# Gathers of the experts' rows on GpSimd: when a group of gathers waits for an earlier group to land

## Chip, core and metric

The kernel runs on one core of a Trainium2 chip. The metric is the device time of one execution in microseconds (us). Three runs of the kernel before gave 585.29 us as their median.

## What is computed

x has 8 sequences of 256 tokens with 128 features, 2048 tokens in all. Four layers are added to x, each on its layer norm: a state-space mixer, a routed feed-forward layer, a selective scan (Mamba), and the same routed feed-forward layer once more. Cut to what matters here:

```
x = x + attn_a(layernorm(x), ...)          # state-space mixer
x = x + ffn(layernorm(x), ...)             # first routed layer, t = 0 in the kernel
x = x + attn_b(layernorm(x), ...)          # selective scan
x = x + ffn(layernorm(x), ...)             # last routed layer, t = 1

def ffn(h):                                # 16 experts, each token takes the best one
    score = sigmoid(max over experts of h @ router.T), only for that expert
    routed = for each token: expert(score * h), expert = silu(gate) * up, then down
    shared = (silu(h @ shared_gate.T) * (h @ shared_up.T)) @ shared_down.T
    return shared + routed
```

## The kernel before

x stays in SBUF as 16 blocks of 128 tokens; four blocks are a group (group 0 to 3). Each engine has its own program, written out by hand in the order in which it runs, and engines wait for one another on named semaphores. Nothing reorders it.

A routed layer (`experts`, once with t = 0 and once with t = 1) goes like this:

- GpSimd (POOL in the profile) scatters each token's scaled row to an HBM tensor `by_expert`, in which the rows of an expert stand together in slots. These are indirect DMAs, one for each block of 128 tokens (`send`, L1821), four in a row for a group.
- SyncE and ScalarE fetch the slots, TensorE runs the experts on them (L736, L751, L763), and the results go back to `by_expert` as SyncE's and ScalarE's DMAs (L1970, L1604).
- When the last of them has landed (`put_back`), GpSimd gathers the rows back into the order of the tokens: 16 indirect DMAs at L1858, one for each block, in the loop `for g in GROUPS`. Each group of four has a semaphore of its own, `read_back[g]`. Before groups 2 and 3 GpSimd waits for the group two ahead (L1856).
- Beside that, the shared part runs. TensorE projects a group to gate and up (`project`, L699), ScalarE takes the gate through silu (L1554), VectorE multiplies it with up (L1178), TensorE projects down (`down`, L712), and VectorE adds the result to x (`add_shared`, L1184). `land` (L1244, VectorE) waits for `read_back[g]` and adds a gathered group to x.

What stands around the gathers differs between the two layers.

- First routed layer, on the way into the scan (`enter_scan`): VectorE does `land(0)`, the layer norm of group 0, `add_shared(2)`, the first piece of the shared part of group 3, `land(1)`, `land(2)` and then the other pieces. TensorE does `down(2)`, the transposes of group 0 (L446), one piece of group 3 (L699), and the 16 matmuls of the scan's input projection (`project_u`, L800), which wait for ScalarE to copy the transposed group (L1426). The last gathered group is added by GpSimd itself in the scan (`land_last`, L1897). Behind the gathers GpSimd has the products of the scan's steps (L1904).
- Last routed layer (`leave`): VectorE does `add_shared(2)`, the pieces of group 3, `land(1)`, `land(2)`, `add_shared(3)`, `land(3)`; SyncE writes a group out after each `land` (L1975). Nothing stands behind the gathers on GpSimd.

Of the kernel before, what the change touches and what calls it, by code (L numbers as in the profile page):

```python
# [15 lines left out]
GB = BANK // P  # L16
# [103 lines left out]
def build(nc, x_in, w_in, c_in, out):  # L120
    with ExitStack() as stack:
# [6 lines left out]
        def signal(name, events, step=1):  # L128
            return Signal(sem(name), events, step)

        pe, dve, act, pool, sp = (Queue(e) for e in (nc.tensor, nc.vector, nc.scalar, nc.gpsimd, nc.sync))
# [18 lines left out]
        def wt(name, rows=slice(0, P)):  # L150
            at, width = W_AT[name]
            return w[rows, at:at + width]
# [5 lines left out]
        def register(engine, place, below):  # L158

            return nc.values_load(place, engines=(engine,), min_val=0, max_val=below - 1,  # L160
                                  skip_runtime_bounds_check_because="the slots of all experts are fewer than the blocks")
# [21 lines left out]
        def blocks(g):  # L183
            return range(GB * g, GB * g + GB)
# [207 lines left out]
        read_back = [signal(f"read_back{g}", [(t, j) for t in TURNS for j in blocks(g)], 16) for g in GROUPS]  # L392
# [1390 lines left out]
        def gpsimd_program():  # L1783
# [17 lines left out]
            def hold_score(n, g):  # L1801

                js = slice(GB * g, GB * g + GB)
                pool.wait_ge(*score_exp[n, g])
                nc.gpsimd.tensor_scalar(score[:, js], score[:, js], 1.0, 3e38, ALU.add, ALU.min).then_inc(*score_held.inc((n, g)))

            def scale_rows(n, g):
                js = slice(GB * g, GB * g + GB)
                pool.wait_ge(*scores_ready[n, g])
                pool.wait_ge(*turned[n, g])  # L1810
                nc.gpsimd.tensor_tensor(xn[:, js, :], xn[:, js, :], score[:, js].unsqueeze(2).to_broadcast([P, GB, DM]),
                                        ALU.mult).then_inc(*rows_scaled.inc((n, g)))

            def send(n, js):

                g = js[0] // GB
                pool.wait_ge(*placed[n, g])
                pool.wait_ge(*rows_scaled[n, g])
                pool.wait_ge(*filled[len(fills) - 1])
                for j in js:  # L1820
                    nc.gpsimd.indirect_dma_start(by_expert, bass.IndirectOffsetOnAxis(position[:, j:j + 1], 0),  # L1821
                                                 xn[:, j, :], None).then_inc(*scatter[n // 2].inc(j))

            def experts(t, entry):
                n = 1 + 2 * t
                hold_score(n, NGRP - 1)
                scale_rows(n, NGRP - 1)
                send(n, blocks(NGRP - 1))
                for mark in entry:
                    pool.wait_ge(*mark)  # L1830

                def choose_weights(k):

                    if k >= 3:
                        pool.wait_ge(*expanded[t, k - 3])
                    s = pairs[k][1]
                    e = register(mybir.EngineType.Pool, expert_int[s:s + 1, 0:1], NE)
                    nc.gpsimd.tensor_copy(chosen[s % len(chosen)], wt("gate_up")[:, bass.ds(e * (2 * EF), 2 * EF)]).then_inc(*second_chosen.inc((t, k)))  # L1838

                whole_pairs = [k for k in range(n_pairs) if len(pairs[k]) == 2]  # L1840
                pool.wait_ge(*expert_ready[t])
                for k in whole_pairs[0:3]:
                    choose_weights(k)
                if t == 0:
                    pool.wait_ge(*taps_loaded[0])
                    pool.wait_ge(*load_late["w"])
                    nc.gpsimd.tensor_tensor(taps, taps, wt("in_b")[:, 0:DI].unsqueeze(1).to_broadcast([P, DC, DI]),
                                            ALU.mult).then_inc(*taps_ready.inc(0))
                    nc.gpsimd.tensor_tensor(past, ident.unsqueeze(1).to_broadcast([P, NCH, P]),
                                            wt("d_b").unsqueeze(2).to_broadcast([P, NCH, P]), ALU.mult).then_inc(*past_ready.inc(0))  # L1850
                for k in whole_pairs[3:]:
                    choose_weights(k)
                pool.wait_ge(*put_back[t][back[-1]])
                for g in GROUPS:
                    if g >= 2:
                        pool.wait_ge(*read_back[g - 2][t, GB * (g - 1) - 1])  # L1856
                    for j in blocks(g):
                        nc.gpsimd.indirect_dma_start(gathered[:, j, :], None, by_expert,  # L1858
                                                     bass.IndirectOffsetOnAxis(position[:, j:j + 1], 0)).then_inc(*read_back[g].inc((t, j)))
# [15 lines left out]
            for g in range(NGRP - 1):  # L1875
                if g >= 1:
                    hold_score(1, g)
                scale_rows(1, g)
                send(1, blocks(g))
            experts(0, exit_a)  # L1880

            def drive(g):
# [16 lines left out]
            for s in range(n_steps + 1):  # L1899
# [9 lines left out]
                for what, g in due_in_steps(s):  # L1909
# [10 lines left out]
                    elif what == "send 1":  # L1920
                        send(3, blocks(g)[1:GB])
            experts(1, exit_b)


# [151 lines left out]
```

## Time and profile before

| what | us |
|---|---|
| median of three runs (lowest, highest) | 585.29 (580.48, 586.97) |
| the profiled execution | 589.76 |
| its span, first to last instruction | 588.4 |
| outside the span | 1.4 |
| TensorE busy in the span | 480.0 (82%) |
| VectorE busy | 407.8 (69%) |
| ScalarE busy | 314.7 (53%) |
| GpSimd busy | 319.8 (54%) |

The mean granted TensorE clock over the span is 0.916 of full speed (2.4 GHz). The table tells how busy an engine is, not what bounds a stretch; for that the stretches with the gathers (205 to 254 us and 550 us to the end) have to be read row by row.

### The profile page before, as it was taken

What the parts mean: (1) busy time and instruction counts of PE and PEld (TensorE: products, weight loads), DVE (VectorE), ACT (ScalarE), POOL (GpSimd) and SP (SyncE); (2) the same over time, 40 slices, a digit from 0 to 9 for tenths busy, and PEclk for the clock granted to TensorE, in tenths of its full rate; (3) what the DMA queues carried; (4) which work ended last, traced back from release to release, by engine and by line L of the source; (5) the groups of instructions that cost most, each with busy time, mean ns of one, the idle gap of its engine ahead of it and who ended that gap; (6) DMA issues with size and microseconds to landing.
All of it is one profiled execution on the core that took longest, in us unless ns stands there. A gap on an engine that the chain in (4) does not pass through costs nothing.

```text
span 588.4 us, 7447 instructions
## 1 busy us (share of the span) xinstructions
PE 480.0 (82%) x2128; PEld 276.2 (47%) x2128; DVE 407.8 (69%) x821; ACT 314.7 (53%) x655; POOL 319.8 (54%) x298
## 2 busy tenths in 40 slices
PE   3987878988789984899788997887778677899936
PEld 1744446565459951363233443333324233489614
DVE  4588692974453333299999799999997997544303
ACT  2573656454435530557665885978386641646200
POOL 1059541553452172046789669897989666411450
PEclk9898996997898996989997998999798899899976
DMA  8999920000033410154555354566465630043321
GB/s 299 410 324 326 319 78 0 2 20 18 19 103 110 122 49 22 43 146 140 160 156 143 111 154 114 163 144 184 112 168 138 161 109 20 19 113 112 85 60 53
DMA packets 39991, 73.94 MB, mean 126 GB/s; under 512 B 4368, under 2 KB 20240, under 8 KB 39184
## 3 DMA queue, kind: packets, MB, share of 16 engines
q1 hardware_dynamic: 35600, 67.00, 38.0%
q0 software_dynamic: 2048, 4.20, 2.5%
q10 hardware_dynamic: 2304, 2.29, 1.2%
q8 instruction: 17, 0.28, 0.2%
q14 instruction: 22, 0.18, 0.1%
HBM read 66.00 MB, written 26.28 MB: 157 GB/s over the span
## 4 chain that ended last, share of the span: by engine, by line
PE 33%; DVE 24%; issue 15%; ACT 12%; POOL 8%; another core or an unknown queue 5%; DMA 2%; SPq 1%; DVEq 0%; POOLq 0%; ACTq 0%
DVE arena L1313 9%; PE psum L699 5%; PE psum L751 5%; POOL arena L1904 4%; PE psum L881 3%; PE psum L712 3%; PE psum L763 2%; PE psum L800 2%; DVE psum L1307 2%; ACT L1391 2%; ACT arena L1712 2%; ACT xn L1421 2%; PE psum L457 1%; POOL by_expert L1821 1%
## 5 line engine op out<-in xcount | busy, mean ns | idle before, releaser
L1904 POOL TENSOR_TENSOR arena<-arena 128x512 f32<-128x512 f32 x127 | 158.3, 1271 | 68.0 <-DVE arena L1313 67.7
L881 PE MATMUL psum<-arena,w 128*128 128x512 f32 x256 | 136.4, 652 | 27.8 <-POOL arena L1904 25.8
L1313 DVE TENSOR_TENSOR_SCAN arena<-arena,psum 128x512 f32<-128x512 f32 x128 | 148.4, 1200 | 8.3 <-ACT arena L1712 4.8
L1712 ACT ACTIVATE arena<-arena 128x510 f32<-128x510 f32 x128 | 87.2, 713 | 41.9 <-DVE arena L1313 39.5
L881 PEld LDWEIGHTS psum<-arena,w 128*128 128x128 f32 x256 | 46.6, 201 | 102.8 <-POOL arena L1904 76.4
L1307 DVE TENSOR_TENSOR psum<-psum,arena 128x512 f32<-128x512 f32 x128 | 81.5, 681 | 1.1 <-DMA arena<-bc_store 1.0
L699 PE MATMUL psum<-xnt,w 128*128 128x512 f32 x128 | 64.2, 651 | 10.2 <-ACT arena L1554 10.2
L1789 POOL TENSOR_TENSOR arena<-arena 128x512 f32<-128x512 f32 x16 | 20.7, 1295 | 69.6 <-DVE arena L1014 69.6
L1858 POOL DMA_INDIRECT arena<-by_expert,routes x32 | 30.6, 956 | 29.8 <-DMA by_expert<-arena 20.6
L699 PEld LDWEIGHTS psum<-xnt,w 128*128 128x128 f32 x128 | 25.5, 208 | 39.4 <-issue 27.5
L1821 POOL DMA_INDIRECT by_expert<-xn,routes x32 | 33.7, 1053 | 14.3 <-issue 7.9
L800 PE MATMUL psum<-xnt,arena 128*128 128x512 f32 (+3 forms) x64 | 33.1, 651 | 9.3 <-ACT xnt L1426 9.3
L1178 DVE TENSOR_TENSOR arena<-psum,arena 128x512 f32<-128x512 f32 x24 | 16.3, 689 | 34.9 <-PE psum L699 21.9
L1554 ACT ACTIVATE arena<-psum 128x512 f32<-128x512 f32 x24 | 14.2, 595 | 43.5 <-PE psum L699 18.4
L1391 ACT ACT_TABLE_LOAD x24 | 30.8, 1283 | 10.5 <-DMA c<-c_in 8.8
L751 PE MATMUL psum<-arena 128*128 128x128 f32 x248 | 34.3, 283 | 2.4 <-issue 2.4
L712 PEld LDWEIGHTS psum<-w,arena 128*128 128x128 f32 x256 | 33.1, 210 | 6.5 <-issue 6.5
L712 PE MATMUL psum<-w,arena 128*128 128x128 f32 x256 | 33.4, 293 | 1.8 <-DVE arena L1178 1.8
L1233 DVE TENSOR_TENSOR arena<-psum,arena 128x256 f32<-128x256 f32 (+1 forms) x32 | 13.3, 416 | 28.5 <-PE psum L763 18.1
L751 PEld LDWEIGHTS psum<-arena 128*128 128x128 f32 x248 | 31.5, 199 | 2.8 <-issue 2.8
L1838 POOL COPY arena<-w 128x256 f32 x30 | 11.8, 402 | 36.6 <-PE psum L751 36.6
L1184 DVE TENSOR_TENSOR x<-psum,x 128x512 f32<-128x512 f32 x7 | 4.8, 689 | 34.5 <-remote 26.2
(199 smaller groups left out, 826.8 us busy)
## 6 DMA issues: line engine op xcount, KB each, us to landing
arena<-bc_store SPq DMA_DIRECT2D x64, 512.0 KB, 4.9
by_expert<-w_in SPq DMA_DIRECT2D x4, 4096.0 KB, 43.4
w<-w_in SPq DMA_DIRECT2D x1, 4427.5 KB, 13.4
by_expert<-arena SPq DMA_DIRECT2D x56, 64.0 KB, 1.6
arena<-by_expert SPq DMA_DIRECT2D x54, 64.0 KB, 2.0
by_expert<-w_in SPq DMA_DIRECT2D x1, 1984.0 KB, 66.8
x<-x_in SPq DMA_DIRECT2D x4, 256.0 KB, 7.5
out<-x SPq DMA_DIRECT2D x4, 256.0 KB
```

The source lines that it names most:

```text
L699: nc.tensor.matmul(b, weights[:, P * c:P * c + P], xnt_group(g), start=True, stop=True).then_inc(*made.inc((t, g, c)))
L712: r = nc.tensor.matmul(b[:, P * q:P * q + P], act_of(t, g)[:, c, P * q:P * q + P], wt("shared_down")[:, DM * c:DM * c + DM], start=(c == 0 ...
L751: r = nc.tensor.matmul(b[:, P * (2 * q + half):P * (2 * q + half) + P], chosen[s % len(chosen)][:, EF * half:EF * half + EF], xs_t[:, P * ...
L800: r = nc.tensor.matmul(by_sequence(b)[:, :, back:SEQ], taps[:, DC - 1 - back, P * c:P * c + P], by_sequence(xnt_group(g))[:, :, 0:SEQ - ba ...
L881: nc.tensor.matmul(bank(6 + c), ident, state[c][s % 3], start=False, stop=(n == DS - 1)).then_inc(*summed.inc((s, c)))
L1307: nc.vector.tensor_tensor(bank(2 + c), bank(c), bc_row[i][:, 0, :], ALU.mult).then_inc(*driven.inc((s, c)))
L1313: nc.vector.tensor_tensor_scan(state[c][s % 3], decay_b[c][s % 2], bank(2 + c), 0.0, ALU.mult, ALU.add).then_inc(*state_ready.inc((s, c)))
L1391: nc.scalar.preload_act_table_set(name)
L1712: nc.scalar.activation(live, seq, ACT.Exp, scale=a_neg[:, DS * c + n:DS * c + n + 1]).then_inc(*decay_ready.inc((s, c)))
L1821: nc.gpsimd.indirect_dma_start(by_expert, bass.IndirectOffsetOnAxis(position[:, j:j + 1], 0), xn[:, j, :], None).then_inc(*scatter[n // 2] ...
L1858: nc.gpsimd.indirect_dma_start(gathered[:, j, :], None, by_expert, bass.IndirectOffsetOnAxis(position[:, j:j + 1], 0)).then_inc(*read_back ...
L1904: nc.gpsimd.tensor_tensor(state[c][s % 3], state[c][s % 3], bc_row[s % len(bc_row)][:, 1, :], ALU.mult).then_inc(*y_done.inc((s, c)))
```

## The change

Two lines of GpSimd's program differ:

```diff
                 for g in GROUPS:
-                    if g >= 2:
-                        pool.wait_ge(*read_back[g - 2][t, GB * (g - 1) - 1])
+                    if g == 2 or (g and t == 0):
+                        pool.wait_ge(*read_back[g - 1][t, GB * g - 1])
                     for j in blocks(g):
```

In the first routed layer each of groups 1, 2 and 3 now waits for the group just ahead of it. In the last one only group 2 waits, for group 1. No instruction is added, removed or moved on any engine but for these waits.

On GpSimd, in the first routed layer, between the last copy of an expert's weights and the first product of the scan; `put_back0` is the landing of the experts' results, `read_back0` to `read_back2` are the landings of gathered groups 0 to 2:

```order
 L1858 DMA arena<-by_expert,routes 128x128 [waits put_back0]
-L1858 DMA arena<-by_expert,routes 128x128 x7
+L1858 DMA arena<-by_expert,routes 128x128 x3
 L1858 DMA arena<-by_expert,routes 128x128 [waits read_back0]
 L1858 DMA arena<-by_expert,routes 128x128 x3
 L1858 DMA arena<-by_expert,routes 128x128 [waits read_back1]
 L1858 DMA arena<-by_expert,routes 128x128 x3
+L1858 DMA arena<-by_expert,routes 128x128 [waits read_back2]
+L1858 DMA arena<-by_expert,routes 128x128 x3
 L1904 TENSOR_TENSOR arena<-arena 128x512 [waits bc_loaded0,state_ready]
```

The wait for group 0 has moved from the ninth gather to the fifth, that for group 1 from the thirteenth to the ninth, and there is a new one for group 2 at the thirteenth.

On GpSimd, in the last routed layer, to the end of its program:

```order
 L1858 DMA arena<-by_expert,routes 128x128 [waits put_back1]
 L1858 DMA arena<-by_expert,routes 128x128 x7
-L1858 DMA arena<-by_expert,routes 128x128 [waits read_back0]
-L1858 DMA arena<-by_expert,routes 128x128 x3
 L1858 DMA arena<-by_expert,routes 128x128 [waits read_back1]
-L1858 DMA arena<-by_expert,routes 128x128 x3
+L1858 DMA arena<-by_expert,routes 128x128 x7
```

Here the ninth gather waits for group 1 (the eight ahead of it) rather than for group 0, and the thirteenth waits for nothing.

## Rows read from the trace of the kernel before

**Rows 1.** The chain that ended last, its shares of the span by engine.
```profile
PE 33%; DVE 24%; issue 15%; ACT 12%; POOL 8%; another core or an unknown queue 5%; DMA 2%; SPq 1%; DVEq 0%; POOLq 0%; ACTq 0%
```
**Rows 2.** The same chain in order of time, its longest pieces: start us, us, what.
```profile
217.58 10.95 another core or an unknown queue
...
556.03 17.36 another core or an unknown queue
```
**Rows 3.** Waits: engine and line, waited for: us in total, times, longest us.
```profile
DVE x L1184 <- remote: 26.2, 2, 15.1
...
ACT arena L1554 <- remote: 16.8, 1, 16.8
...
ACT xnt L1426 <- remote: 11.0, 1, 11.0
```
**Rows 4.** TensorE in order of time, first routed layer: start us, us, what [idle before <-releaser].
```profile
213.94 3.81 PE L712 MATMUL psum<-w,arena 128*128 128x128 f32 x32 [0.88 <-DVE arena L1178]
217.58 0.60 PE L446 MATMUL psum<-w,xn 128*128 128x128 f32 x4
218.02 1.88 PE L699 MATMUL psum<-xnt,w 128*128 128x512 f32 x4
229.21 9.91 PE L800 MATMUL psum<-xnt,arena 128*128 128x512 f32 x16 [9.30 <-ACT xnt L1426]
```
**Rows 5.** VectorE and ScalarE in order of time, first routed layer.
```profile
228.50 0.69 DVE L1184 TENSOR_TENSOR x<-psum,x 128x512 f32<-128x512 f32 x1 [11.07 <-remote]
...
228.56 0.60 ACT L1426 ACTIVATE xnt<-psum 128x512 f32<-128x512 f32 x1 [10.97 <-remote]
```
**Rows 6.** GpSimd in order of time, first routed layer: gathers 1, 9 and 16.
```profile
205.68 1.02 POOL L1858 DMA_INDIRECT arena<-by_expert,routes  x1 [8.89 <-DMA by_expert<-arena]
...
215.84 0.95 POOL L1858 DMA_INDIRECT arena<-by_expert,routes  x1 [0.30 <-issue]
...
224.65 0.95 POOL L1858 DMA_INDIRECT arena<-by_expert,routes  x1 [0.30 <-issue]
```
**Rows 7.** GpSimd in order of time, last routed layer: gathers 4, 8 and 16.
```profile
554.38 0.95 POOL L1858 DMA_INDIRECT arena<-by_expert,routes  x1 [0.30 <-issue]
...
559.40 0.95 POOL L1858 DMA_INDIRECT arena<-by_expert,routes  x1 [0.30 <-issue]
...
569.43 0.95 POOL L1858 DMA_INDIRECT arena<-by_expert,routes  x1 [0.30 <-issue]
```
**Rows 8.** VectorE in order of time, last routed layer.
```profile
556.96 0.69 DVE L1244 TENSOR_TENSOR x<-x,arena 128x512 f32<-128x512 f32 x1 [1.11 <-DMA arena<-by_expert,routes]
557.57 0.68 DVE L1178 TENSOR_TENSOR arena<-psum,arena 128x512 f32<-128x512 f32 x1
573.37 0.69 DVE L1184 TENSOR_TENSOR x<-psum,x 128x512 f32<-128x512 f32 x1 [15.12 <-remote]
...
585.43 0.69 DVE L1244 TENSOR_TENSOR x<-x,arena 128x512 f32<-128x512 f32 x1
```
**Rows 9.** TensorE in order of time, last routed layer.
```profile
556.67 3.73 PE L712 MATMUL psum<-w,arena 128*128 128x128 f32 x32
560.24 3.60 PE L699 MATMUL psum<-xnt,w 128*128 128x512 f32 x8
...
578.72 5.88 PE L712 MATMUL psum<-w,arena 128*128 128x128 f32 x32 [0.88 <-DVE arena L1178]
```
**Rows 10.** The scatters, whole span: line engine op, count | busy us, mean ns | idle before.
```profile
L1821 POOL DMA_INDIRECT by_expert<-xn,routes x32 | 33.7, 1053 | 14.3 <-issue 7.9
```
**Rows 11.** GpSimd in order of time: the third group of four scatters, its first and last.
```profile
150.06 1.06 POOL L1821 DMA_INDIRECT by_expert<-xn,routes  x1 [1.62 <-DVE routes L1002]
...
153.97 0.97 POOL L1821 DMA_INDIRECT by_expert<-xn,routes  x1 [0.30 <-issue]
```
**Rows 12.** Stretches: us, busy PE PEld DVE ACT POOL, clock, DMA share, GB/s.
```profile
220.00:228.00 8.00, 0.00 (x0) 0.00 (x0) 0.00 (x0) 0.00 (x0) 4.39 (x5) 0.79 0.20 49
228.00:236.00 8.00, 6.79 (x10) 2.90 (x11) 5.07 (x20) 1.34 (x3) 0.00 (x0) 0.57 0.00 0
```

## The prediction

> **What bounds the kernel now.** I read the page first. The busy shares name TensorE, but the chain that ended last holds a term that belongs to no engine: 5% of the span is put down to "another core or an unknown queue" [rows 1]. On one core that is strange. In order of time almost all of it is two pieces, 10.95 us from 217.58 and 17.36 us from 556.03 [rows 2], and both lie inside the two stretches in which GpSimd issues its 16 gathers, 205.68 to 225.60 and 550.57 to 570.38 [rows 6, 7]. The list of waits has only three lines that end "remote", and they are the same two places [rows 3].
>
> Then the first stretch engine by engine. TensorE ends `down(2)` at 213.94 + 3.81 = 217.75 and the transposes of group 0 at 218.18 [rows 4]. VectorE's `add_shared(2)` waits for nothing but that `down(2)`, and ScalarE's copy for nothing but those transposes; they start at 228.50 and 228.56 [rows 5]. So 10.7 and 10.4 us pass between the end of the work and the start of whoever waits for it. From 220 to 228 TensorE, VectorE and ScalarE run no instruction at all, while GpSimd goes on; the DMA engines are busy for only 0.20 of the time [rows 12]. The second stretch is a copy of it: TensorE ends `down(2)` at 560.40 and runs eight more matmuls to 563.84 [rows 9]; VectorE's L1184 starts at 573.37 [rows 8], 13.0 us after its input.
>
> What do the two have in common? Both are let go a fixed time after the gathers: 228.50 is 2.90 us after the last gather's end in the first layer (224.65 + 0.95 = 225.60), 573.37 is 2.99 us after it in the last (569.43 + 0.95 = 570.38). A gather lands about 2.58 us after its start: the fourth gather starts at 554.38 and `land(0)`, which waits for it, starts at 556.96 [rows 7, 8]. So the release comes 1.3 to 1.4 us after the last landing. My reading: **while a long unbroken train of gathers runs, TensorE's signals reach nobody**, and they are given out when the train has drained. When it sets in can be bounded. TensorE's result at 556.8 (L699, just before the `down` of rows 9) still reached VectorE at 557.57 [rows 8], when six gathers had been started; the result at 560.40 did not come through, with the eighth just done and the ninth due at 560.65. In the first layer the result at 217.75 was held, after gather 9 at 215.84 [rows 6].
>
> Trains of four show nothing of the kind. The 32 scatters are the same kind of instruction of the same length, 1053 ns [rows 10], in groups of at most four with several us between groups (one is 150.06 to 154.94 [rows 11]); no wait in the whole profile ends "remote" beside them [rows 3].
>
> **The change, part by part.** The old waits never bind: gather 9, which has one, follows at the usual 0.30 us [rows 6]. So nothing is gained from their removal. A new wait binds each time, as the group just ahead has not landed. Gathers stand 1.26 us apart ((224.65 - 205.68) / 15); with a wait the next one starts 2.58 us plus about 0.07 us after the one ahead. Each new wait costs GpSimd 2.65 - 1.26 = 1.4 us: 4.2 us for three in the first layer, 1.4 us for one in the last.
>
> Who stands behind it? In the first layer the landings become: group 0 at 209.46 + 2.58 = 212.0 (unchanged), group 1 at 218.5, group 2 at 225.0, group 3 at 231.4. Group 3 is for `land_last` and GpSimd's first scan product, in the scan, which begins later in any case. Group 2 is for VectorE's `land(2)`.
>
> What a break does to the hold is shown by no row, so it is bounded from both sides. Lower end: a drained queue starts the count afresh, trains of four behave as the scatters do, and the hold is gone. Upper end: the hold ignores 1.4 us breaks and lasts until 1.3 us after the last landing. I take the first, since trains of four are the nearest rows; the second stays in the range.
>
> *First layer without the hold.* The copy of the transposes starts at 218.2 and takes 0.60; TensorE is busy with L699 to 219.90; then come the 16 matmuls of L800. They took 9.91 us at a granted clock of 0.57 of full speed [rows 4, 12]: TensorE had idled since 219.90, and the clock had fallen from 2.4 to 1.2 GHz. At full clock eight 512-column matmuls take 3.60 us with their tail, 0.43 us each [rows 9], so 16 take 6.9 us. They end at 219.9 + 6.9 = 226.8, not at 229.21 + 9.91 = 239.12: **12.3 us earlier**. Is VectorE late then? `land(2)` waits for 225.0 and is done with its layer-norm sums by about 227.0; its next task needs TensorE's L699 behind L800, 227 to 228.5. It is just in time, so the whole way into the scan moves by 12.3 us.
>
> *Last layer without the hold.* `add_shared(2)` starts at 560.4 and the pieces of group 3 follow each other: (3,1) and (3,2) are projected by 563.84, the last piece two matmuls later (1.7 us for both halves at full clock), its silu and product 1.3 us: `down(3)` can start near 566.5 and takes 3.73 us at full clock [rows 9], where it took 5.88 at the lower level. `add_shared(3)` would be done at 571. Now the gathers are what is late: gather 8 lands at 559.40 + 2.58 = 561.98, gather 9 starts at 562.05, gather 16 at 562.05 + 7 x 1.26 = 570.9, and lands at 573.5. `land(3)` starts then and not at 585.43 [rows 8]: **11.9 us earlier**, of which the wait itself has taken 1.4 back.
>
> If only the release in the middle works there, and the hold sets in again at the end of the second train, `down(3)` is given out near 573.5 + 1.4 = 574.9 and `land(3)` starts near 575.6: 9.8 us earlier instead.
>
> Sum in the profiled execution: 589.76 - 12.3 - 11.9 = 565.6 us. That execution is 4.5 us above the median of the runs (589.76 - 585.29), so against the median 585.29 - 24.2 = **561.1 us**; with the smaller term for the last layer 563.2. I say 562.
>
> **A rule that speaks against it.** The waits keep GpSimd from starting transfers it could start, which the rows price at 5.6 us in all. The Trainium skill, page "DMA: Bandwidth & Descriptors", section "Rules for kernel authors", says the opposite of what is done here: issue a DMA early and wait on its semaphore late, so that the fixed cost overlaps. By that rule alone the kernel gets slower, which is rival 1. The page "SBUF — State Buffer", section "SBUF: two separate sides", adds that a DMA cannot slow a compute engine nor the reverse. The 8 us without an instruction on three engines beside running gathers [rows 12] don't fit a world in which nothing couples them, though it is their signals and not their ports that seem held. No page read says that a signal of TensorE can be held.
>
> **Rivals.**
>
> 1. *The hold stays and ends later (slower).* It is not the length of the train but its being there at all that holds TensorE's signals, once begun, until the last gather has landed. For it: both releases stand at the same distance from the last gather's end, and no row shows a break that released anything. Against it: trains of four. Price: +4.2 us where the held result goes out at 232.7, +1.4 us at the end: 585.29 + 5.6 = 590.9. It decides from the point at which a drained queue of 1.4 us does not reset the hold.
> 2. *Only the first layer is cured.* The last layer keeps trains of eight, and the hold set in somewhere between the sixth gather and the ninth. If it comes by the eighth and a break doesn't lift it, the last layer pays 1.4 us and the first wins 12.3: 585.29 - 12.3 + 1.4 = 574.4.
> 3. *The hold belongs to the profiled execution only.* Then the timed runs never lost it, the first layer changes nothing and the last pays the wait where the gathers bound its end: 585.29 + 1.4 = 586.7. Against it: without holds of 24 us in sum the runs would lie near 562, and the lowest is 580.48. A change that does nothing would look the same in the result.
>
> **How the numbers follow.** Both layers cured 0.50 (558 to 567 as its own range: the two sums, and the 3 us by which a run of before leaves the median); first layer only 0.17 (570 to 578); hold stays 0.21 (588 to 593); profile only, or no effect, 0.12 (584 to 588). The predicted time is that of the first. The range has to reach over the second and into the third: 558 to 591 leaves out about 0.15. A measurement of this kernel tells about 1% (5.9 us) from no change. Faster by over 1%: 0.67, the first two cases. Rival 1 stands at the edge, +0.96%, so I give half of it to slower, 0.10; the rest and rival 3 are within 1%, 0.23.
>
> **What would show it right or wrong.** In the changed profile the gathers should stand in trains of four with gaps of about 1.7 us idle in the first layer, and in two trains of eight in the last. The "remote" waits of VectorE L1184, ScalarE L1426 and L1554 should be gone, L800 should start near 220 and end near 227 at full clock, and the last L1244 should start 2.6 us after gather 16 and end on a gather's landing rather than on L712. If L1184 still starts some 2.9 us after the last gather's end, rival 1 holds; if that is so only in the last layer, rival 2; if the waits are gone in the profile and the time hasn't moved, rival 3. The forecast is wrong in size if `land(2)` or something else on VectorE turns out later than L800.

## The result and the profile after

The change made the kernel faster: six runs of the changed kernel gave a median of 566.16 us (563.34 to 572.51), six of the kernel before on the same chip 584.74 us (579.95 to 586.97). The ratio is 0.9688, with a 95% interval of 0.9627 to 0.9749; it leaves out the changed kernel's one slow run, that of 572.51 us. The forecast was 562.0 us in a range of 558 to 591. Two later comparisons gave 0.9669 [0.9604, 0.9734] and 0.9654 [0.9605, 0.9703]. But in three other sessions (a session is one batch of runs on one chip, with the kernel before timed beside the others) the kernel before itself ran at 561 to 563 us, with nothing for the change to win. That is the main thing that the experiments found, and it comes below.

The changed profiled execution took 568.88 us, its span is 567.5. Its chain by engine, against [rows 1]:

```profile
PE 38%; DVE 22%; issue 16%; POOL 10%; ACT 10%; DMA 3%; another core or an unknown queue 1%; ACTq 0%; POOLq 0%; DVEq 0%
```

The term that belonged to no engine has gone from 5% to 1%. Of the three "remote" lines of [rows 3] one is left, and its one wait is 4.4 us, not 15.1:

```profile
DVE x L1184 <- remote: 4.4, 1, 4.4
```

GpSimd in order of time, first routed layer, gathers 4 to 6, 8, 9, 12 and 13 (for [rows 6]), columns as there:

```profile
213.32 0.95 POOL L1858 DMA_INDIRECT arena<-by_expert,routes  x1 [0.30 <-issue]
216.16 1.28 POOL L1858 DMA_INDIRECT arena<-by_expert,routes  x1 [1.89 <-DMA arena<-by_expert,routes]
217.75 0.95 POOL L1858 DMA_INDIRECT arena<-by_expert,routes  x1 [0.30 <-issue]
...
220.27 0.95 POOL L1858 DMA_INDIRECT arena<-by_expert,routes  x1 [0.30 <-issue]
223.08 1.28 POOL L1858 DMA_INDIRECT arena<-by_expert,routes  x1 [1.86 <-DMA arena<-by_expert,routes]
...
227.18 0.95 POOL L1858 DMA_INDIRECT arena<-by_expert,routes  x1 [0.31 <-issue]
230.13 1.28 POOL L1858 DMA_INDIRECT arena<-by_expert,routes  x1 [2.00 <-DMA arena<-by_expert,routes]
```

The trains of four are there, with 1.86 to 2.00 us of idle time between them, each ended by a landing, and the first gather behind a break takes 1.28 us and not 0.95. TensorE, VectorE and ScalarE beside them (for [rows 4, 5]):

```profile
215.19 3.81 PE L712 MATMUL psum<-w,arena 128*128 128x128 f32 x32 [0.88 <-DVE arena L1178]
219.71 0.66 PE L446 MATMUL psum<-w,xn 128*128 128x128 f32 x4 [0.71 <-issue]
...
221.92 6.99 PE L800 MATMUL psum<-xnt,arena 128*128 128x512 f32 x16
```
```profile
219.57 0.68 DVE L1184 TENSOR_TENSOR x<-psum,x 128x512 f32<-128x512 f32 x1
```
```profile
220.40 0.60 ACT L1426 ACTIVATE xnt<-psum 128x512 f32<-128x512 f32 x1 [0.59 <-issue]
```

`down(2)` ends at 219.00. L1184 starts at 219.57, when VectorE has done its own work ahead of it, and no longer 10.7 us behind its input. L800 starts with no wait and takes 6.99 us, as TensorE's clock never fell. The stretch that was empty on three engines in [rows 12] is now full on TensorE, at 2.4 GHz:

```profile
222.00:230.00 8.00, 8.00 (x20) 3.52 (x19) 2.74 (x11) 1.57 (x3) 4.14 (x4) 1.00 0.14 38
```

The last layer, TensorE and then VectorE (for [rows 8, 9]):

```profile
547.45 3.73 PE L712 MATMUL psum<-w,arena 128*128 128x128 f32 x32
551.02 5.32 PE L699 MATMUL psum<-xnt,w 128*128 128x512 f32 x12
557.22 3.81 PE L712 MATMUL psum<-w,arena 128*128 128x128 f32 x32 [0.88 <-DVE arena L1178]
```
```profile
552.14 0.69 DVE L1184 TENSOR_TENSOR x<-psum,x 128x512 f32<-128x512 f32 x1 [3.75 <-PE psum L712]
...
563.75 0.69 DVE L1184 TENSOR_TENSOR x<-psum,x 128x512 f32<-128x512 f32 x1 [4.45 <-remote]
564.55 0.69 DVE L1244 TENSOR_TENSOR x<-x,arena 128x512 f32<-128x512 f32 x1
```

and GpSimd, gathers 8, 9, 15 and 16:

```profile
549.51 0.95 POOL L1858 DMA_INDIRECT arena<-by_expert,routes  x1 [0.30 <-issue]
552.38 0.94 POOL L1858 DMA_INDIRECT arena<-by_expert,routes  x1 [1.91 <-DMA arena<-by_expert,routes]
...
560.43 0.95 POOL L1858 DMA_INDIRECT arena<-by_expert,routes  x1 [0.31 <-issue]
561.68 0.95 POOL L1858 DMA_INDIRECT arena<-by_expert,routes  x1 [0.30 <-issue]
```

With trains of eight the hold (the time for which TensorE's result is kept from whoever waits for it) is not gone, it is short. `down(2)` ends at 547.45 + 3.73 = 551.18 and its L1184 starts at 552.14, 1.0 us late, just as gather 8 lands (the chain puts that landing at 552.11). `down(3)` ends at 561.03, with the seventh gather of the second train under way, and its L1184 starts at 563.75, 2.7 us late. Here that costs next to nothing, as gather 16 lands at about 564.3 and the last L1244 needs it.

The trace also dates the updates of the semaphores, and they tell what it is that comes late. In the kernel before, TensorE's four results of 217.75, 218.18, 219.04 and 219.90 raised their semaphores at 228.47, 228.53, 228.58 and 228.62, one right behind the other, while landings of gathers were recorded up to 227.03. The second of these is the end of the first piece of [rows 2], 217.58 + 10.95. ScalarE starts 0.03 us after it [rows 5]. So VectorE and ScalarE did not miss a signal that was there; the signal was late.

### The profile page after: what moved, and what is told of

Same layout as the page of the kernel before. It is cut to its first block, busy times and chain, and to the rows that moved or that the text cites. A ratio compares the mean times of both kernels' runs of the same rounds, so it can differ in the third digit from the quotient of the medians.

```text
span 567.5 us, 7447 instructions
## 1 busy us (share of the span) xinstructions
PE 478.4 (84%) x2128; PEld 276.4 (49%) x2128; DVE 410.5 (72%) x821; ACT 314.9 (55%) x655; POOL 320.0 (56%) x298
## 2 busy tenths in 40 slices
DMA packets 39991, 73.94 MB, mean 130 GB/s; under 512 B 4368, under 2 KB 20240, under 8 KB 39184
## 4 chain that ended last, share of the span: by engine, by line
PE 38%; DVE 22%; issue 16%; POOL 10%; ACT 10%; DMA 3%; another core or an unknown queue 1%; ACTq 0%; POOLq 0%; DVEq 0%
DVE arena L1313 10%; PE psum L699 7%; PE psum L751 5%; POOL arena L1904 4%; PE psum L712 4%; PE psum L881 3%; PE psum L763 3%; DVE psum L1307 2%; PE psum L800 2%; PE psum L685 2%; ACT arena L1712 2%; POOL arena L1858 2%; ACT xn L1421 2%; ACT L1391 2%; PE psum L680 1%
## 5 line engine op out<-in xcount | busy, mean ns | idle before, releaser
L1712 ACT ACTIVATE arena<-arena 128x510 f32<-128x510 f32 x128 | 87.2, 713 | 42.3 <-DVE arena L1313 39.9
L1307 DVE TENSOR_TENSOR psum<-psum,arena 128x512 f32<-128x512 f32 x128 | 81.4, 681 | 1.0 <-DMA arena<-bc_store 0.9
L699 PE MATMUL psum<-xnt,w 128*128 128x512 f32 x128 | 62.6, 639 | 0.0
L1858 POOL DMA_INDIRECT arena<-by_expert,routes x32 | 32.1, 1002 | 37.9 <-DMA by_expert<-arena 22.3
L699 PEld LDWEIGHTS psum<-xnt,w 128*128 128x128 f32 x128 | 25.4, 207 | 29.2 <-issue 28.3
L1821 POOL DMA_INDIRECT by_expert<-xn,routes x32 | 31.8, 995 | 13.5 <-issue 8.0
L751 PE MATMUL psum<-arena 128*128 128x128 f32 x248 | 33.1, 276 | 2.4 <-issue 2.4
L712 PEld LDWEIGHTS psum<-w,arena 128*128 128x128 f32 x256 | 31.5, 202 | 5.7 <-issue 5.7
L712 PE MATMUL psum<-w,arena 128*128 128x128 f32 x256 | 31.9, 285 | 1.8 <-DVE arena L1178 1.8
L1233 DVE TENSOR_TENSOR arena<-psum,arena 128x256 f32<-128x256 f32 (+1 forms) x32 | 13.3, 416 | 26.0 <-PE psum L763 18.3
L751 PEld LDWEIGHTS psum<-arena 128*128 128x128 f32 x248 | 30.2, 192 | 2.8 <-issue 2.8
L800 PE MATMUL psum<-xnt,arena 128*128 128x512 f32 (+3 forms) x64 | 30.5, 607 | 0.0
L446 PE MATMUL psum<-w,xn 128*128 128x128 f32 x64 | 11.5, 314 | 15.6 <-ACT xn L1421 10.3
```

Of the source, the lines that this page charges most:

```text
L699: nc.tensor.matmul(b, weights[:, P * c:P * c + P], xnt_group(g), start=True, stop=True).then_inc(*made.inc((t, g, c)))
L712: r = nc.tensor.matmul(b[:, P * q:P * q + P], act_of(t, g)[:, c, P * q:P * q + P], wt("shared_down")[:, DM * c:DM * c + DM], start=(c == 0 ...
L751: r = nc.tensor.matmul(b[:, P * (2 * q + half):P * (2 * q + half) + P], chosen[s % len(chosen)][:, EF * half:EF * half + EF], xs_t[:, P * ...
L800: r = nc.tensor.matmul(by_sequence(b)[:, :, back:SEQ], taps[:, DC - 1 - back, P * c:P * c + P], by_sequence(xnt_group(g))[:, :, 0:SEQ - ba ...
L1307: nc.vector.tensor_tensor(bank(2 + c), bank(c), bc_row[i][:, 0, :], ALU.mult).then_inc(*driven.inc((s, c)))
L1712: nc.scalar.activation(live, seq, ACT.Exp, scale=a_neg[:, DS * c + n:DS * c + n + 1]).then_inc(*decay_ready.inc((s, c)))
```

## The experiments

The time from the end of TensorE's `down` to the start of its L1184 gives the hold its length in each profile; without a hold it is 0.04 us where VectorE is free. Six sessions, and in each the kernel before was timed beside the experiments:

| session | kernel before, median (runs) | what was run in it | hold in its profiles |
|---|---|---|---|
| 1 | 584.74 us (6) | the changed kernel | kernel before: 10.7 and 13.0 us; changed kernel: 1.0 and 2.7 us, last layer |
| 2 | 562.79 us (25) | e1, e2, e3, e4 | none |
| 3 | 586.08 us (7) | e5, e6, e7 | e5: 10.9 and 11.9 us; e7: 13.1 and 12.2 us; e6: 0.5 and 2.5 us, last layer |
| 4 | 560.98 us (13) | e8, e9, e10 | none |
| 5 | 561.92 us (9) | e11 | none |
| 6 | 584.11 us (11) | e12 | changed kernel: 1.8 us, last layer |

No session mixed the two: all runs of the kernel before were above 579 us in sessions 1, 3 and 6, and below 569 in 2, 4 and 5. Sessions 3 and 4 have the same chip number, 0, in their results.

The traces differ in one more thing. A DMA's landing raises its semaphore 16 times, and the trace records each update: 64 for a group of four gathers, 4368 in the whole kernel. All eight traces of sessions 2, 4 and 5 have the full 4368. All six of sessions 1, 3 and 6 have fewer: 3812 to 3819 in the kernel before and e7, 3901 to 3969 in the changed kernel. In the kernel before 372 of the 512 updates of its 32 gathers are missing, in the changed kernel of session 1 195, and 145 to 169 of the scatters' in each of the six. The page shows it in small: where each transfer of a group lacks updates it gives no time to landing. This is its line of the output's DMAs in the kernel before, and then in e1 (session 2):

```profile
out<-x SPq DMA_DIRECT2D x4, 256.0 KB
```
```profile
out<-x SPq DMA_DIRECT2D x4, 256.0 KB, 2.7
```

So holds and missing records of semaphore updates come together: both in six traces, neither in the other eight. Whether one brings about the other, or a third thing both, no run tells. One rival has to be kept in mind with all that follows: that recording the updates has a part in the hold. Every run on record has its span and granted clock from the profiler, so none shows an execution that wasn't recorded.

**e1, e2, e3, e4: where the waits stand.** The edits at L1855, each against the changed kernel. The last fence has two: e3 takes the line marked e3, e4 the one marked e4.

```diff
-                    if g == 2 or (g and t == 0):                       # e1
-                        pool.wait_ge(*read_back[g - 1][t, GB * g - 1])
```
```diff
-                    if g == 2 or (g and t == 0):                       # e2
+                    if g and t == 0:
                         pool.wait_ge(*read_back[g - 1][t, GB * g - 1])
+                    if g >= 2 and t == 1:
+                        pool.wait_ge(*read_back[g - 2][t, GB * (g - 1) - 1])
```
```diff
-                    if g == 2 or (g and t == 0):
+                    if g:                                              # e3
+                    if g == 2:                                         # e4
```

> Both layers gather 16 blocks in one train with no wait at all. Theory A (the hold on TensorE's signals comes from a long unbroken train and ends when it has drained): the same as the kernel before, 585 us, with L1184 starting some 13 us after its down in the last layer. Theory B (the hold comes from a gather that carries a wait for a landing while other gathers are in flight, as the ninth and thirteenth did before): no hold, 562 to 566 us. A tells from B by about 20 us.

> The change in the first layer alone, the last layer as before. If the two layers are cured independently, the last layer keeps its hold and loses the 11.7 us that it won: 584.7 - 11.5 = 573 us; the profile shows L1184 of the last layer about 3 us behind the last gather's end and none of it in the first layer.

> Trains of four in the last layer too: two more waits there, each 1.6 to 2.0 us of GpSimd time by the first layer of the changed kernel. Theory A: the short holds of the last layer vanish, but the gathers bound its end, so 566.2 + 3.6 = 569.8 us. If instead the short holds cost more than the waits, below 566.

> Trains of eight in both layers. Theory A: in the first layer down(2) ends about 9.5 us after the first gather's start, while the first train of eight (10.1 us, landing at about 11.4) is still running; a hold then lasts until that train has landed, at most 2 us, and the scan's entry is late by as much: 566 to 569 us. If a train of eight does not reach the point where the hold sets in, 565 to 566 us.

Measured: e1 562.61 us, ratio 1.0032 [0.9979, 1.0084]; e2 563.38 us, 0.9997 [0.9958, 1.0037]; e4 563.08 us, 1.0003 [0.9962, 1.0044]; e3 569.88 us, 1.0123 [1.0054, 1.0192]. By the letter of e1's expectation theory B had won, but the kernel before stood at 562.79 us, so nothing could be told of a hold: there was none to be had. e3 came out at the 569.8 us that was expected of it, but by chance: that was worked out for a session with the hold, as 3.6 us on top of 566.2, and here it is 7.1 us on top of 562.79. This is VectorE and TensorE of e1 in the first layer, where gather 10 of an unbroken train starts at 214.07 and gather 16 at 221.63:

```profile
210.70 3.81 PE L712 MATMUL psum<-w,arena 128*128 128x128 f32 x32 [0.87 <-DVE arena L1178]
```
```profile
214.55 0.69 DVE L1184 TENSOR_TENSOR x<-psum,x 128x512 f32<-128x512 f32 x1 [0.36 <-PE psum L712]
```

The input is ready at 214.51 and taken at 214.55. What the session did tell is the price of the waits without a hold. From the start of `down(1)` to the last L1244's end the last layer takes 26.5 us in e1, 26.0 in e2, 26.8 in e4 (which has the changed kernel's waits there) and 31.5 in e3. From `down(1)` to the scan's first L1307 the first layer takes 37.4 us in e1, e2 and e4 alike, though e2 has the change's three waits. (It takes 38.3 in e3, whose gathers began 4.0 us after `down(1)` and not 1.5 to 1.8.) So in these profiles the change's waits cost nothing in the first layer and 0.3 to 0.8 us in the last, and three waits in the last layer cost 5.0 to 5.5: there the gathers set the end.

**e5, e6, e7: is the hold in the kernel or in the session?** e5 is the kernel before, e6 the changed kernel, e7 is e1 again, all unedited.

> The kernel before, unchanged, profiled again. In the last comparison its timed runs came to 562.8 us where they had been 584.7. If the hold belongs to the chip or session and not to the kernel, the profile shows it or not together with the time: near 585 us with L1184 some 11 and 13 us behind its down, or near 560 us with L1184 right behind it in both layers. If the hold were in every execution, it would be there also at 562 us.

> The changed kernel, unchanged, beside the kernel before. Where the kernel before stands near 585 us (hold there): a ratio near 0.97. Where it stands near 562 us (no hold): the breaks only cost, about 0.5 us at the end of the last layer, a ratio of 1.000 to 1.005.

> All 16 gathers of a layer with no wait among them. If the kernel before shows a hold in this job: theory A (long train) wants it here as well, near 585 us; theory B (a gather that carries a wait) wants none, near 562 us. If the kernel before shows no hold here, this one shows none either, 558 to 563 us.

Measured: kernel before 586.08 us; e5 587.04 us in its one run, e6 566.68 us (565.24 to 568.54), ratio 0.9669, e7 580.02 us in its one run. The waits of e7:

```profile
DVE x L1184 <- remote: 27.6, 2, 15.0
ACT arena L1554 <- remote: 16.0, 1, 16.0
ACT xnt L1426 <- remote: 12.5, 1, 12.5
```

and its first layer, TensorE, VectorE, GpSimd (gathers 8 and 16):

```profile
207.48 3.81 PE L712 MATMUL psum<-w,arena 128*128 128x128 f32 x32 [0.88 <-DVE arena L1178]
```
```profile
224.43 0.69 DVE L1184 TENSOR_TENSOR x<-psum,x 128x512 f32<-128x512 f32 x1 [12.62 <-remote]
```
```profile
210.56 0.95 POOL L1856 DMA_INDIRECT arena<-by_expert,routes  x1 [0.30 <-issue]
...
220.60 0.95 POOL L1856 DMA_INDIRECT arena<-by_expert,routes  x1 [0.30 <-issue]
```

The same program that had no hold in session 2 has one of 224.43 - 211.29 = 13.1 us here, and it ends 2.88 us behind the last gather's end (221.55), as in the kernel before. No gather waits for a landing in it. Theory B falls: the hold does not need waits. Theory A stands for the sessions that have a hold. That e7 is 6 us below the kernel before is not the hold's doing: from `down(1)` on it takes 51.0 us to the scan and 36.6 us at the end, where e5 takes 50.1 and 36.6; it was 6.8 us ahead when `down(1)` started, before the first gather.

The same trace tells something of whose signals are held. VectorE's layer norm and the transposes of TensorE that wait for it:

```profile
210.70 1.12 DVE L964 TENSOR_SCALAR xn<-x,moments,rstd 128x128 f32<-128x128 f32 x4 [0.60 <-issue]
```
```profile
211.87 0.66 PE L446 MATMUL psum<-w,xn 128*128 128x128 f32 x4 [0.58 <-issue]
```

VectorE's result is there at 211.82 and TensorE goes on at 211.87, while TensorE's own result of 211.29 is held until 224.43. So at that moment TensorE's signals were held and VectorE's signal to TensorE was not.

**e8: whose signals are held?** On the kernel before, ahead of the two held instructions:

```diff
                 scale(2, 0)
+                for r in range(RALLY):
+                    if r:
+                        dve.wait_ge(*returns[r - 1])
+                    nc.vector.memset(served, 0.0).then_inc(*serves.inc(r))
+                dve.wait_ge(*returns[RALLY - 1])
                 add_shared(2)
...
                 table_set(SILU)
+                for r in range(RALLY):
+                    act.wait_ge(*serves[r])
+                    nc.scalar.activation(returned, served, ACT.Copy).then_inc(*returns.inc(r))
                 take_turned(2, 0)
```

> The kernel before, with 16 rounds of a tiny fill on VectorE and a tiny copy on ScalarE that wait for each other, put right ahead of the two instructions that were held in the first layer (L1184 and L1426). A round is worth some 0.4 us, so 16 take 6 to 7 us, and they start as gather 9 or 10 is issued. If only TensorE's signals are held, the rally runs at its own pace inside the hold, ends near 225 us on the old time line, and L1184 still starts about 3 us behind the last gather's end: no time added. If every engine's signals are held, the first round stalls until the release and the rest comes behind it: 6 to 7 us added. On a chip without the hold the rally itself costs 6 to 7 us.

The session had no hold (kernel before 560.98 us). The rally took 0.42 us a round and 6.7 us in all. The one run took 569.57 us, 8.6 above the median of the kernel before where 6 to 7 were expected; its gathers also began later, 4.7 us after `down(1)`. Of the hold it tells nothing. What is known is the one signal of e7 at the start of a hold; later in it VectorE and ScalarE had nothing to send, since both waited for TensorE, and so for the rest of a hold the question stays open.

**e9, e10, e11: rate or length?** e9 and e11 are one kernel without waits for landings:

```diff
-                    if g >= 2:
-                        pool.wait_ge(*read_back[g - 2][t, GB * (g - 1) - 1])
...
+                        if j < NBLK - 1:
+                            nc.gpsimd.tensor_copy(spacer, ident).then_inc(*pool_steps.inc())
+                            pool.wait_ge(*pool_steps.now())
```

e10 is e4 again.

> No wait for a landing among the gathers; instead GpSimd does a small copy after each of them, so that they stand some 1.8 us apart and not 1.26, and the train never pauses long enough to be empty for long. Theory A1 (the hold comes when no quiet moment occurs in a long train): it is there as in the kernel before, and as the train is 8 us longer, the time is above it, 590 us or more. Theory A2 (a backlog: signals of landings come faster than they are taken, and TensorE's wait behind them): a lower rate leaves no backlog, no hold, and the last layer's end follows the longer train: 566 to 572 us. On a chip without the hold: 566 to 570 us against 563.

> Trains of eight in both layers, again, now hoped for on a chip with the hold. There the last layer of the changed kernel showed two short holds with trains of eight (about 0.5 to 0.9 us and 2.4 to 2.7 us). In the first layer down(2) ends near the start of the eighth gather, so a hold of up to about 3 us is expected, until that train has landed: 1 to 3 us above the changed kernel's 566.5 us. If the time is at or below 566.5, trains of eight are as good in the first layer.

> The spaced gathers again, in the hope of a session in which the kernel before stands near 585 us. There: theory A1 (no quiet moment in a long train) 590 us or more, with L1184 held until some 3 us behind the last gather; theory A2 (a backlog that a lower rate avoids) 570 us, as in the session without the hold. If the kernel before stands near 562 us again, this tells nothing new and should repeat 569.6 us.

Both sessions were without a hold. Spaced gathers (1.6 us apart, not the 1.8 expected) came to 569.56 us, ratio 1.0101 [1.0023, 1.0179], and again to 566.46 us, 1.0069 [1.0014, 1.0125]; half-way waits in both layers to 565.45 us, 1.0062 [1.0014, 1.0111], where the session of e4 had shown 1.0003 for the same kernel. So spacing cost 0.7 to 1.0%; whether half-way waits cost anything is not settled; and what either would spare in a session with a hold wasn't seen. Rate against length stays open, and so does whether trains of eight would do in the first layer.

**e12: the changed kernel once more.** Unedited.

> The changed kernel against the kernel before once more, since three sessions have now shown the kernel before at 561 to 563 us and the change itself was never timed in one of these. Session with the hold (before near 585): ratio 0.967 again. Session without it (before near 562): the waits only cost. Bounds from the rows: at least the 1.6 us by which gather 16 of the last layer starts later, less the slack there, so 0.5 us; at most what trains of four in both layers cost, 1.2%. I expect a ratio of 1.000 to 1.008.

The kernel before stood at 584.11 us and the changed one at 563.86 us: 0.9654 [0.9605, 0.9703]. By its time of 584.11 us the kernel before had the hold, and the change took it away a third time. In its profile trains of eight again leave a short hold at the end of the last layer: `down(3)` ends at 552.10 + 3.81 = 555.91 and L1184 starts at 557.73.

```profile
552.10 3.81 PE L712 MATMUL psum<-w,arena 128*128 128x128 f32 x32 [0.88 <-DVE arena L1178]
```
```profile
557.73 0.69 DVE L1184 TENSOR_TENSOR x<-psum,x 128x512 f32<-128x512 f32 x1 [4.33 <-remote]
```

The changed kernel itself was never timed in a session without a hold. From e1, e2 and e4 I would expect it 0.3 to 0.8 us slower there than the kernel before, as an estimate, which none of these comparisons could tell from nothing.

## Why the prediction was right, and where not

*The mechanism.* Right in its first reading, for the sessions that have a hold: TensorE's signals are held beside a long unbroken train of gathers, and breaks for a landing keep the hold away. e7 shows that the hold comes without any wait among the gathers. The point at which it sets in can be drawn closer. In e12's last layer a result of TensorE at 542.50 was taken at 542.54, when the seventh gather had started at 542.26; in the changed kernel of session 1 a result at 561.03 was held, when the seventh of its second train had started at 560.43. And a drained queue does reset it, which no row had shown: three breaks in the first layer, no hold. What couples a train to TensorE's signals, no run shows.

*The first layer, 12.3 us.* From the start of `down(1)` to the scan the kernel before took 49.8 us and the changed one 38.4: 11.4 us. L800 took 6.99 us where 6.9 were worked out. The 0.9 us short are in the row of L446: the first gather started 3.8 us later in this execution, so `land(0)` was at 215.92 and the transposes waited 0.71 us for the layer norm behind it. In e12 the gathers of the changed kernel began 1.9 us after `down(1)` and not 4.1, and the first layer took 37.4 us.

*The wait's price, 1.4 us.* Too small. The break is 2.84, 2.81 and 2.95 us from start to start, not 2.65, and the gather behind it takes 0.33 us more: groups stand 6.69, 6.92 and 7.05 us apart where unbroken ones stand 5.06, so 1.6 to 2.0 us each. So `land(2)` came at 229.89 and not at 225.0, the later start included. It was not just in time: VectorE was done with it at 231.8, when its next input, from L699 behind L800, had been ready since 230.63. That cost nothing all the same, and that was luck, as the sum had no such slack in it: without a hold `land(2)` came 21.9 us after `down(1)` in e2 and 18.3 in e1, and both reached the scan after 37.4.

*The last layer, 11.9 us.* From `down(1)` to the last L1244's end: 39.9 us before, 28.2 after, so 11.7. But this term depended on the execution it was read from. In e5, the second profile of the kernel before, that stretch took 36.6 us: there the last `down` ran in 3.81 us at 2.4 GHz, not in the 5.88 us of [rows 9] at the lower clock, and the gathers began 3.2 us after `down(1)` and not 4.3. Against e6's 28.0 us the gain is 8.6 us. This is the term that was mis-sized for the typical execution. The sum of 24.2 us was too large by more than that: the three measured differences of the medians are 18.6, 19.4 and 20.2 us, and the spans of the two profiled pairs differ by 20.9 (588.4 to 567.5) and 18.5 (585.7 to 567.2), of which the two layers make 23.1 and 20.3. The rest lies outside both layers: in both pairs the changed kernel started `down(1)` of the first layer later, by 1.2 and 2.2 us, where the programs are the same. That is half of the rest in the first pair and all of it in the second.

*Rivals.* Rival 1 (the hold ignores breaks) was wrong. Rival 2 had a grain of truth: trains of eight do reach the point where the hold sets in, but the break lifts it, and the landing that is waited for hides the rest. Rival 3 (the profiled execution only) was wrong as put, but its neighbour was missing from the list: that the hold may be absent from the whole session. The argument against it, that the runs would lie near 562 us without holds, was sound, and in three sessions they did lie there. I had taken three runs of one session as what the kernel does. That the result was measured in a session with the hold was luck: in one of the others a time near 562 us might have come out all the same, as e2 and e4 did at 563, but none of the gain of 24.2 us.

*The rule that spoke against.* Of the waits alone it was right where they stand on gathers that bound the end: without a hold e3's cost 1.2%. e4 and e10, one kernel, came out at nothing and at 0.6%. That is the rule of the Trainium skill, page "DMA: Bandwidth & Descriptors", section "Rules for kernel authors", to issue early and wait late; e3 agrees with it in a session without a hold, and in the sessions with one the measurement decides against it.

## What to carry to other kernels

On a one-core program a wait that the profile puts down to "remote" is a question to follow up: take the end of the instruction that must have released it, the start of the one that waited, and look at what stops when it is let go. If a long train of GpSimd's indirect DMAs stands there, try a wait for a landing after every four, placed where nobody waits for the last gather: it costs 1.6 to 2.0 us of GpSimd's time each and took 11 us of standstill away, in sessions that have a hold. In the others there is nothing to win. Look also whether the trace has all its semaphore updates (a missing time to landing is a sign). And time both kernels in the same session, and in more than one, before a gain is called the kernel's own.

## What the runs showed of the hardware that was not expected

- In some sessions, and by their times in all executions of these, TensorE's results reach neither VectorE nor ScalarE while a train of gathers 1.26 us apart runs on, from about the seventh on. They were held for up to 13.1 us and let go 2.9 to 3.2 us after the last gather's end. In other sessions the same programs with the same gathers show nothing of it, and the medians of the kernel before are 21 to 25 us lower.
- The traces with a hold lack 399 to 556 of the 4368 semaphore updates of landing DMAs; those without a hold lack none. What makes a session the one or the other was not found, nor whether an execution that isn't recorded has the hold.
- Groups of four, scatters or gathers, showed no hold, though updates of theirs are missing too; trains of eight showed 0.1 to 2.7 us.
- With three breaks in the first layer, one gather behind each break, the first or the second, takes 1.24 to 1.42 us and not 0.95 (session 1, e2, e3, e6, e12). With one break in each layer (e4, e10) none does.
